# Moving a PSUM copy from VectorE to ScalarE, and two small products ahead of two long ones, in a transformer layer on eight cores

## The reference, cut to what matters

```python
x = x + attn(layernorm(x), Wq, Wk, Wv, Wo)      # rope, 16 heads, 4 kv heads, causal, softmax
x = x + ffn(layernorm(x), gate_w, mask_up_w, gate_proj_w, up_proj_w, down_proj_w, inv_map)

# ffn: N tokens, hidden H = 2048, inner I = 1408, G = 8 groups
soft = softmax(where(flat == 0, NEG_INF, flat))              # from the router, top 8
xg = x[:, None, :] + einsum('ngi,ghi->ngh', soft, mask_up_w) # input of group g
g_ = einsum('ngh,gih->ngi', xg, gate_proj_w)
u  = einsum('ngh,gih->ngi', xg, up_proj_w)
d  = einsum('ngi,ghi->ngh', silu(g_) * u, down_proj_w)
y  = einsum('ng,ngh->nh', scalar, d)                         # summed over the groups
```

## Time and profile before

| what | value |
|---|---|
| median of 3 runs | 3502.54 us (3501.1 to 3809.34) |
| the profiled execution, its own time | 3501.65 us |
| its span (slowest core, core 5) | 3500.1 us |
| spans of the eight cores | 3488.7 to 3500.1 us |
| mean granted TensorE clock of the cores | 0.898 to 0.903 |
| busy: PE, DVE, ACT, POOL | 84%, 31%, 11%, 11% of the span |
| stage 1 | about 27 to 241 us of the span |
| stage 4, groups | about 1414 to 3455 us |

### The profile page before, as it was taken

The page is one execution under the profiler, slowest core; times in us unless marked ns, Lnnn a source line. Parts: engine busy times, 40 slices in busy tenths (PEclk is TensorE's granted clock), DMA queues, the critical chain, the costliest instruction groups (busy, mean ns, idle before and its releaser), DMA issues.

```text
span 3500.1 us, 34199 instructions; the slowest of 8 cores (3488.7 to 3500.1 us)
## 1 busy us (share of the span) xinstructions
PE 2950.7 (84%) x12602; PEld 1313.2 (38%) x12602; DVE 1080.2 (31%) x1390; ACT 401.1 (11%) x631; POOL 385.0 (11%) x350
## 2 busy tenths in 40 slices
PE   1347787788765998799999999999999999999986
PEld 1222332122233447243443443443443433434434
DVE  3542234443452115413213214123123123122113
ACT  1210011233453110000000000000000000000000
POOL 0000010000000100111111111111111111111110
PEclk9997898555687995799999999999999999999998
DMA  5211255000002630777676686676775876776745
GB/s 126 81 46 19 24 49 57 1 1 13 1 1 66 79 31 1 69 76 69 65 77 66 64 81 62 65 77 63 72 73 56 82 71 58 73 74 64 74 45 122
DMA packets 640647, 200.52 MB, mean 57 GB/s; under 512 B 632027, under 2 KB 632540, under 8 KB 639206
## 3 DMA queue, kind: packets, MB, share of 16 engines
q0 software_dynamic: 628208, 159.67, 47.4%
q1 hardware_dynamic: 12278, 38.67, 3.4%
HBM read 349.57 MB, written 8.39 MB: 102 GB/s over the span
## 4 chain that ended last, share of the span: by engine, by line
PE 73%; DVE 9%; DMA 9%; issue 5%; ACT 3%; DVEq 0%; SPq 0%; ACTq 0%; POOLq 0%
PE PS L1198 17%; PE PS L1204 17%; PE PS L1249 13%; DMA AR<-downT 7%; PE PS L531 3%; PE PS L757 3%; DVE AR L768 3%; PE PS L858 2%; PE PS L762 2%; PE PS L480 2%; PE PS L382 2%; PE PS L425 2%; PE PS L949 2%; PE PS L706 1%; DMA AR<-x_perm 1%
## 5 line engine op out<-in xcount | busy, mean ns | idle before, releaser
L1198 PE MATMUL PS<-AR 128*128 128x512 bf16 x2816 | 841.1, 380 | 16.5 <-DVE AR L1165 16.5
L1204 PE MATMUL PS<-AR 128*128 128x512 bf16 x2816 | 840.5, 380 | 0.0
L1249 PE MATMUL PS<-AR 128*128 128x512 bf16 x2816 | 646.4, 387 | 39.7 <-DMA AR<-downT 30.6
L1249 PEld LDWEIGHTS PS<-AR 128*128 128x128 bf16 x2816 | 270.4, 99 | 415.5 <-issue 122.6
L1223 DVE TENSOR_TENSOR AR<-PS,AR 128x1024 bf16<-128x1024 f32 x88 | 107.8, 1225 | 1025.4 <-ACT AR L1218 1025.4
L1198 PEld LDWEIGHTS PS<-AR 128*128 128x128 bf16 x2816 | 275.6, 98 | 353.1 <-issue 24.2
L1204 PEld LDWEIGHTS PS<-AR 128*128 128x128 bf16 x2816 | 276.3, 98 | 334.8 <-issue 4.5
L1261 DVE TENSOR_TENSOR AR<-AR,PS 128x1024 f32<-128x1024 f32 x128 | 156.3, 1221 | 458.8 <-PE PS L1249 455.5
L1218 ACT ACTIVATE AR<-PS 128x1024 bf16<-128x1024 f32 x88 | 90.1, 1023 | 1810.4 <-PE PS L1204 1810.4
L757 PE MATMUL PS<-AR 128*128 128x384 bf16 (+3 forms) x365 | 159.5, 438 | 106.4 <-DVE AR L745 105.0
L736 ACT ACTIVATE AR<-PS,AR 128x384 bf16<-128x384 f32 (+3 forms) x365 | 197.6, 576 | 305.4 <-PE PS L706 128.3
(11 more groups left out here) (124 smaller groups left out, 1857.1 us busy)
## 6 DMA issues: line engine op xcount, KB each, us to landing
AR<-gateT POOLq DMA_DIRECT2D x88, 512.0 KB, 6.4
AR<-upT POOLq DMA_DIRECT2D x88, 512.0 KB, 8.2
AR<-downT POOLq DMA_DIRECT2D x128, 352.0 KB, 5.3
AR<-x_perm SPq DMA_DIRECT2D x48, 512.0 KB, 3.7
AR<-Wq POOLq DMA_DIRECT2D x16, 512.0 KB, 7.4
AR<-Wo POOLq DMA_DIRECT2D x16, 512.0 KB, 6.3
out<-AR SPq DMA_DIRECT2D x8, 1024.0 KB, 3.9
AR<-Wk POOLq DMA_DIRECT2D x4, 512.0 KB, 9.2
```

Of the source, the lines that this page charges most:

```text
L1198: fn = (lambda t_, hh=hh, tc=tc, psG=psG, sl=sg: nc.tensor.matmul(psG[:, tc * 512:(tc + 1) * 512], GSL[sl][:, hh * 128:(hh + 1) * 128], XG ...
L1204: fn = (lambda t_, hh=hh, tc=tc, psU=psU, sl=su: nc.tensor.matmul(psU[:, tc * 512:(tc + 1) * 512], USL[sl][:, hh * 128:(hh + 1) * 128], XG ...
L1249: fn = (lambda t_, it=it, tc=tc, psD=psD, sl=sd: nc.tensor.matmul(psD[:, tc * 512:(tc + 1) * 512], DSL[sl][:, it * 128:(it + 1) * 128], AP ...
```

## The change

Two edits. First, in stage 1, the copy out of PSUM is made by ACT (`s_.copy`) in place of DVE. The counts that others wait for change with it, from VE to SE: PE's wait before it overwrites PS[2 + hc], and the key product's wait for XLN. DVE's own wait for the transposes (line 389) stays in the code, now ahead of DVE's next instruction. Second, in stage 4, the small matmuls and additions of pieces 14 and 15 of XG are appended behind down step 13, ahead of down steps 14 and 15.

```diff
@@ -376,8 +376,8 @@
             ps = PS[2 + hc]
-            if evac_done:
-                p.wait("te", "VE", evac_done[-2] if len(evac_done) >= 2 else 0)
+            if len(evac_done) >= 2:
+                p.wait("te", "SE", evac_done[-2])
@@ -387,13 +387,14 @@
             p.wait("ve", "TE", te_norm_free[par])
-            ev = p.inc("ve", lambda v, ps=ps, hc=hc, tt=tt: v.tensor_copy(
+            p.wait("se", "TE", te_norm_free[par])
+            ev = p.inc("se", lambda s_, ps=ps, hc=hc, tt=tt: s_.copy(
                 out=XLN.rearrange("p (hh q) -> p hh q", q=2048)[:, hc * 8:hc * 8 + 8,
                     tt * 128:(tt + 1) * 128],
-                in_=ps.rearrange("p (a b) -> p a b", b=128)), "VE")
+                in_=ps.rearrange("p (a b) -> p a b", b=128)), "SE")
             evac_done.append(ev)
@@ -419,7 +420,7 @@
                 if c == 0:
-                    p.wait("te", "VE", evac_done[(tc * 4 + 3) * 2 + 1])
+                    p.wait("te", "SE", evac_done[(tc * 4 + 3) * 2 + 1])
@@ -1262,7 +1263,11 @@
             if g + 1 < G:
-                emit_xg_hh(g + 1, hh)
+                if hh < 14:
+                    emit_xg_hh(g + 1, hh)
+                    if hh == 13:
+                        emit_xg_hh(g + 1, 14)
+                        emit_xg_hh(g + 1, 15)
```

More of the change, by code:

```diff
@@ L389, in build @@
             p.wait("ve", "TE", te_norm_free[par])
-            ev = p.inc("ve", lambda v, ps=ps, hc=hc, tt=tt: v.tensor_copy(
+            p.wait("se", "TE", te_norm_free[par])
+            ev = p.inc("se", lambda s_, ps=ps, hc=hc, tt=tt: s_.copy(
                 out=XLN.rearrange("p (hh q) -> p hh q", q=2048)[:, hc * 8:hc * 8 + 8,
                     tt * 128:(tt + 1) * 128],
-                in_=ps.rearrange("p (a b) -> p a b", b=128)), "VE")
+                in_=ps.rearrange("p (a b) -> p a b", b=128)), "SE")
             evac_done.append(ev)
     p1a_te = p.cnt["TE"]; p1a_ve = p.cnt["VE"]
-    taps_avail["XLN"] = (XLN, BF16, "VE", p.cnt["VE"])
+    taps_avail["XLN"] = (XLN, BF16, "SE", p.cnt["SE"])
     q_rope_done = kv_rope_done = 0
```

## The result

The changed kernel takes 3468.4 us in the median of ten runs, against 3504.3 us for the kernel before, run beside it. In four of the ten executions before and one of the ten after, a die ran at a lower granted clock; without these the ratio is 0.9911, 95% interval 0.9894 to 0.9929: 0.9% faster, 31 us by the ratio. The forecast was 3474 us, 27.8 us less than the profiled execution before. The gain is inside the 2% that the forecast named as the measure of no change, and clear of zero.

What follows compares the result with a forecast made beforehand. PE was taken as the bound (73% of the span), with at most 196 us of its waits winnable. 3501.65 - 21.8 (edit 1) - 6.0 (edit 2) = 3473.9, say 3474 us; own range 3466 to 3483, 8 in 10 3461 to 3488.

Steps and rivals of the forecast that it cites:

- Edit 1: Stage 1, copy moved to ACT: tile period from 13.26 to 11.91 us, 21.8 us gained in all.
- the ACT branch: Stage 1, tile end: second copy, then next tile's sums on ACT; L339 starts at 9.63, 0.92 us behind DVE's readiness.
- the first rival: Stage 1: the ACT branch does not bind, DVE alone sets a period of 10.99 us; 3460 us, chance 0.10.
- It takes 3.11 us from the start of L372 until its transposes are handed on: Stage 1: time per half, applied to both halves, so the second's transposes are handed on at 6.22 us.
- The dear copy on ACT: Stage 1, rival 3: ACT's strided copy is slow, at 3.68 us the whole takes 3522 us; chance 0.02.
- I take 1.01: Stage 1: assumed time in us of ACT's copy with strided output, with 1.23 kept as the dear end.
- rival 3: Stage 1: the strided copy is dear on ACT; at 3.68 us, period 15.15 and 3522 us, slower; chance 0.02.
- Edit 2: Stage 4, pieces 14 and 15 earlier: stall moves and one pair lies inside it; 6.0 us gained, between 0 and 8.
- up to 0.2 more for each: Stage 4: possible extra gain in us per group end if a down step's ends cost less when another follows.
- The clock at a stall: Stage 4: clock loss after PE's stall, 1.5 us seen once; change put at nothing, far end 10 us.
- the new stall is of the same kind as the old one: Stage 4: the new 1.9 us stall resembles the old 2.14 us wait, so the clock term was left at nothing.
- Rivals 2 and 4: 2: stage 4, old stall stays beside the new, 3494 us, chance 0.10; 4: attention's clock falls, 3518 us at 0.58, chance 0.05.

Runs made afterwards that it cites:

- e4_sums_first: Changed kernel with the next tile's two sums put ahead of this tile's two copies in ACT's queue; ratio 0.9870 to the kernel before.
- e5_no_left_wait: Changed kernel without DVE's wait for PE that was left behind each half's transposes in stage 1; 3471.3 us.
- e6_both: Changed kernel with the next tile's sums ahead of the copies on ACT and DVE's left wait for PE removed; 3432.4 us.
- e9_two_waits: Kernel before with a second, long satisfied wait (for a DVE count) on DVE's copy out of PSUM; 3510.2 us.
- e3_spread: Changed kernel with XG pieces 12 and 13 behind down step 12, 14 and 15 behind 13, so no pair waits; ratio 0.9834 to the kernel before.
- e8_halves_spread: e6_both with the normalized half's buffer chosen by half, not tile, and the last XG pieces spread so no pair waits; 3375.7 us, ratio 0.9619.

## Why the prediction was right

**Edit 1: right in mechanism and nearly in size, 21.8 forecast, 19.2 measured.** The end of a tile is the ACT branch, which the first rival denied: L339 idles 0.68 us behind L328, and the period is 12.01, not 10.99. The steps: the first half takes 3.26 us where I had 3.11, since I carried the start of the DVE copy (one wait) over to an instruction with three; the second 3.10 to ACT's copy (3.11); 0.90 to the sums (0.92); 2.50 to L339 (2.49); 2.25 to the next L372 (2.28). The term that was off is "It takes 3.11 us from the start of L372 until its transposes are handed on", as it was applied to the second L372: 0.15 us in each of 15 tiles, 2.3 of the 2.6 us. The same price stands in front of L334 and makes DVE's branch 0.14 us later too, which is most of why L339 idles 0.68 us and not 0.9.

**The dear copy on ACT: did not come.** 1.01 us with the strided output, the same as the contiguous copy of the earlier trace rows. The step "I take 1.01" held, and rival 3 falls. The rule of the Trainium skill ("ScalarE: Activation LUTs", Rules for kernel authors) that simple elementwise work belongs on VectorE names relu, max, min, add and mul, and its factor is for bf16. For this copy of fp32 out of PSUM the order is the other way: 1.01 us on ACT against 1.23 on DVE.

**Edit 2: right in sign and mechanism, 6.0 forecast, 8.5 measured on average (3 kernels against 5, as above).** The stall moved as described, 2.74 us between the pairs of 13 and 15. Where neither place met the lower level, the stretch from the pair of 13 to the gate product is now 12.77 us, where I had 13.09: the two down steps in a row take 10.03 us with the pair ahead of them, not 10.35, the "up to 0.2 more for each" that I left out of the sum. Before, the same stretch took 13.87 us on the mean of the 56 group ends, small waits for weights included (13.74 by the forecast's sum of the earlier trace rows). That is 1.10 us a group end, 7.7 us in all, where I had 6.0 with the weights. The rest up to 8.5 is inside the scatter of the stage.

**The clock at a stall: the term stood at nothing, and nothing it is.** The reason given, that the new stall is of the same kind as the old one, held: 60 of 112 group ends meet the lower level with the old order, 63 of 112 with the new, about 1.7 us each (1.5 read in the earlier trace rows; the full pace of 0.43 us a pair, which the earlier trace rows ends too early to show, is there in the trace, the next pair starting at 2190.97). What one row could not tell is how often; it is more than half. Had the new stall been kept out of it, or the old one, the term would have been 7 x 0.55 x 1.7 = 6.5 us. The spread pieces, which have neither, show it.

**Rivals 2 and 4: not seen.** The gate product's wait is gone. Attention has a granted clock of 0.64 in this window, as before, so its stage was not slower:

```profile
570.00:1125.00 555.00, 414.86 (x1391) 150.53 (x1417) 224.56 (x507) 213.01 (x380) 0.00 (x0) 0.64 0.07 18
```

The errors offset each other, and that the whole came out so near is in part luck: 2.6 us too much in stage 1, 2.5 too little in stage 4. The two stages give 19.2 + 8.5 = 28 us; what is left to the measured 31 is inside the interval of the ratio, 25 to 37 us.

## What to carry to other kernels

Moving a copy to an idle engine is worth only what its queue allows: look at what stands behind it there, since work that used to run in the shadow now waits in line. Where two branches of nearly one length end a ring, remove both before judging either, as 0.74 and 0.08 us became 3.34 here. And a stall that is moved moves with all that hangs on it, its clock loss too; placing work so that its buffer has long been free took both away.

## What the hardware showed that I had not expected

A stall of 1.7 us on PE is enough for the lower level, in about half of the cases: 63 of 112 group ends in two kernels, with the rest at full pace, and no instruction differs between them. The three further kernels with this order (`e4_sums_first`, `e5_no_left_wait`, `e6_both`) have 32, 28 and 33 of 56, 156 of 280 in all; behind the wait of 2.14 us it is 91 of 168 with `e9_two_waits` (31 of 56). The loss is about 1.7 us each time, as much as the stall. When PE waits for nothing, it did not occur there in 112 cases (`e3_spread`, `e8_halves_spread`). What decides between the two outcomes of one stall is not shown.

Each further wait in front of a DVE instruction on which DVE stands idle starts it 0.07 us later, though its count is long reached (2.30, 2.37 and 2.44 us of idle time before the instruction).

The granted clock that a window shows has to be read beside the pace of the instructions. The windows of stage 1 show 1.00 in the kernel before and in the change. But the view also counts as 1.00 a time for which the trace has no record of the clock, and in both kernels the first record comes only behind the start of the key product (at 243.4 and 224.0 us on the slowest cores). `e8_halves_spread`, core 4, has both kinds of stretch:

```profile
36.00:100.00 64.00, 33.67 (x148) 30.36 (x149) 45.15 (x111) 44.07 (x75) 0.00 (x0) 1.00 0.52 148
106.80:130.70 23.90, 13.27 (x60) 11.76 (x58) 17.28 (x45) 16.36 (x28) 0.00 (x0) 0.50 0.53 173
...
126.33 3.65 PE L394 MATMUL PS<-AR 128*128 128x128 f32 x16 [3.22 <-DVE AR L384]
133.19 2.80 PE L394 MATMUL PS<-AR 128*128 128x128 f32 x16 [3.22 <-DVE AR L384]
```

The first window has no record, the second lies in one of 0.50, and the transposes at 133.19 begin in a record of 1.00 (130.7 to 134.1). Sixteen transposes take 3.65 us in the first two stretches, and 2.80 where the first 0.9 us lie in the record of 1.00. The eight transposes of a half take 1.94 us in every tile of the two kernels, and the key product's first matmuls start 0.43 us apart on all eight cores of both, where 0.22 is the full pace. So PE did its transposes in stage 1 at the lower of its two levels, and a mean like 0.86 for the whole of stage 1 in `e8_halves_spread` (0.58 to 0.86 on the eight cores) is no measure of the level there, nor does it show a slower PE than the 1.00 of the other two.
